# One gather per natural tile and a destination part expanded from h in a graph network kernel

## The reference

```
h = relu(layernorm(x))
fwd = [h[dst], h[src], ea];  bwd = [h[src], h[dst], ea]      # 80 features
msg = relu([fwd; bwd] @ Wf1 + bf1) @ Wf2 + bf2
flow[dst] += msg of fwd;  flow[src] += msg of bwd
x = x + relu(flow @ Wn1 + bn1) @ Wn2 + bn2
h = relu(layernorm(x))
out = x + segment_sum(h[dst], src)
```

## Time and profile before

| | us |
|---|---|
| median of 3 runs | 7432.28 (7426.3 to 7452.46) |
| the profiled execution | 7458.13 |
| its span, first to last instruction | 7456.5 |
| start, to the first DVE work on an edge tile | 186.4 |
| edge stage | 4310.6 |
| record sums | 808 |
| node network | 105 |
| neighbour sums | 2046 |

### The profile page before, as it was taken

The page is one execution under the profiler, slowest core; times in us unless marked ns, Lnnn a source line. Parts: engine busy times, 40 slices in busy tenths (PEclk is TensorE's granted clock), DMA queues, the critical chain, the costliest instruction groups (busy, mean ns, idle before and its releaser), DMA issues.

```text
span 7456.5 us, 123779 instructions
## 1 busy us (share of the span) xinstructions
PE 5573.1 (75%) x24859; PEld 4715.3 (63%) x24860; DVE 3152.5 (42%) x14104; ACT 933.8 (13%) x3532; POOL 5306.1 (71%) x5865
## 2 busy tenths in 40 slices
PE   4898989898989999989898998999833333333334
PEld 3677767677777777767777778999723333333334
DVE  4444444444444444444444445666522232223223
ACT  2111111111111111111111113444200000000000
POOL 0777777777777777777777776666267777777774
PEclk8766676766666666676666665555555555555555
DMA  5111111111111111111111113333121111111111
GB/s 143 43 42 42 42 42 42 42 42 42 42 42 42 41 41 41 41 41 41 41 41 41 41 41 71 73 71 73 21 23 15 14 15 15 14 15 15 15 14 18
DMA packets 916520, 294.53 MB, mean 39 GB/s; under 512 B 795687, under 2 KB 864597, under 8 KB 915822
## 3 DMA queue, kind: packets, MB, share of 16 engines
q0 software_dynamic: 156896, 189.98, 10.1%
q1 hardware_dynamic: 759102, 91.68, 9.0%
q10 hardware_dynamic: 336, 11.20, 0.5%
HBM read 227.82 MB, written 82.32 MB: 42 GB/s over the span
## 4 chain that ended last, share of the span: by engine, by line
POOL 56%; issue 28%; PE 6%; DVE 5%; DVEq 2%; DMA 2%; POOLq 1%; ACT 0%; ACTq 0%; SPq 0%
POOL t L663 19%; POOL records L612 18%; POOL g L602 18%; DVE acc L1186 3%; PE bank L947 1%; PE bank L1002 1%; DVEq L318 1%; DVE oht L1255 1%; DVE ohd L1255 1%; PE bank L809 1%; PE bank L972 1%; PE bank L895 1%; PE bank L894 1%; DVEq L1186 0%; DMA rec_i<-by_d_sd 0%
## 5 line engine op out<-in xcount | busy, mean ns | idle before, releaser
L602 POOL DMA_INDIRECT g<-t_rows,rec_i x1664 | 1615.6, 971 | 625.7 <-issue 505.6
L612 POOL DMA_INDIRECT records<-rec,pos x1664 | 1671.7, 1005 | 518.0 <-issue 501.7
L663 POOL DMA_INDIRECT t<-h_rows,didx x1568 | 1491.0, 951 | 603.8 <-issue 475.6
L1002 PE MATMUL bank<-t,ohd 128*128 x1664 | 376.2, 402 | 1315.1 <-DMA t<-h_rows,didx 1315.1
L893 PE MATMUL bank<-g,ident 128*128 128x128 f32 x3328 | 926.0, 373 | 376.6 <-DMA g<-t_rows,rec_i 376.4
L1002 PEld LDWEIGHTS bank<-t,ohd 128*128 128x128 f32 x1664 | 362.9, 330 | 1328.0 <-issue 1327.8
L895 PE MATMUL bank<-t,oht 128*128 x3328 | 1136.9, 438 | 0.0
L894 PE MATMUL bank<-wee,eaT 17*128 17x128 f32 x3328 | 1120.4, 429 | 0.0
L1195 DVE TENSOR_TENSOR prod<-bank,q_row 128x392 f32<-128x392 f32 x416 | 235.7, 567 | 2086.5 <-PE bank L910 2085.1
L893 PEld LDWEIGHTS bank<-g,ident 128*128 128x128 f32 x3328 | 738.7, 274 | 397.8 <-issue 396.6
L1186 DVE TENSOR_TENSOR acc<-acc,bank 128x65 f32 x3328 | 733.8, 220 | 513.8 <-issue 325.3
(11 more groups left out here) (203 smaller groups left out, 6492.0 us busy)
## 6 DMA issues: line engine op xcount, KB each, us to landing
t<-records SPq DMA_DIRECT2D x104, 536.0 KB, 4.2
rec_i<-by_d_sd SPq DMA_DIRECT2D x1664, 1.0 KB
eaT<-by_d_ea SPq DMA_DIRECT2D x1664, 8.0 KB
g<-t_rows,rec_i POOLq DMA_INDIRECT x1664
records<-rec,pos POOLq DMA_INDIRECT x1664
t<-h_rows,didx POOLq DMA_INDIRECT x1568
by_d_ea<-in_ea ACTq DMA_DIRECT2D x7, 1562.5 KB, 22.1
t_rows<-t2s SPq DMA_DIRECT2D x26, 256.0 KB, 2.3
```

Source lines behind the costliest of these rows:

```text
L602: nc.gpsimd.indirect_dma_start(out=g2[:, r, u, :], out_offset=None, in_=t2_rows, in_offset=bass.IndirectOffsetOnAxis(ap=rec_i[:, r, u, 0:1 ...
L612: nc.gpsimd.indirect_dma_start(out=records, out_offset=bass.IndirectOffsetOnAxis(ap=pos[:, r, u:u + 1].bitcast(U32), axis=0), in_=rec[:, r ...
L663: nc.gpsimd.indirect_dma_start(out=h2g[:, w * W + t, :], out_offset=None, in_=h2_rows, in_offset=bass.IndirectOffsetOnAxis(ap=didx[:, k, t ...
L1002: ins = nc.tensor.matmul(s_bank[r][:, u * D:(u + 1) * D], s_oh[r][:, u, :], h2g[:, bass.ds(at[r * U + u], 1), :].rearrange("p a f -> p (a ...
```

## The change

- t1 is gone. The normalised h is kept as three bf16 parts beside each other (h3, 96 columns for a node: the rounded value, the rounded rest, the rounded rest of that). A new step, expand, multiplies the transposed one-hot with the block of h3; ACT copies the 96 rows from PSUM into rows 0 to 95 of cmb, whose other rows are a row of ones and the 16 edge features. One product cmb x w3 then gives the destination part, the bias and the edge part.
- t2 rows are gathered by the natural tiles (1568) with indices loaded for a whole window (sidx) into a ring of 128 tiles; hidden reads a tile from its slot in the ring.
- The destination one-hot is made by DVE in bf16, by four instructions instead of one, and transposed by PE in bf16. ACT copies it to f32 for sums.
- PE transposes round r + 2 at the end of round r; before it transposed round r + 1 behind hidden of round r.
- x is loaded first from an array laid out by the host, and normalised before the work on the edges; the histogram is moved among the tables; 28 small weight loads become 7; ACT starts the copy of the edge features before the tables, in pieces of 125 elements instead of 1000.
- The neighbour sums are added to x itself, and the copy of x before that stage (L778) is gone.

The diff, cut:

```diff
+H3 = 3 * D
+RG = 8 * W
+NTW = TW
...
-        t1 = sb("t1", [P, NBP, P])
+        h3 = sb("h3", [P, NBP, H3], BF16)
+        ring_flat = sb("ring", [P, RG * P])[:, :]
+        ring = ring_flat.rearrange("p (t c) -> p t c", c=P)
...
-        g2 = sb("g2", [P, R, U, P])
+        sidx = sb("sidx", [P, 8, W, 2], I32)
+        ohd_h = sb("ohd_h", [P, 2, U, P], BF16)
...
-            def load_edges(i, first, last):
+            def load_sources(i, m):
+                sp.dma_start(sidx[:, m, :, :], by_d_sd[bass.ds(i * (W * P), W * P), :].rearrange("(t p) k -> p t k", p=P)).then_inc(ld_nat[m], 16)
+
+            def load_edges(i, m, first, sources):
+                if sources:
+                    load_sources(i + 1, (m + 1) % 8)
...
-            def gather_t2(i, r):
-                pool.wait_ge(ld_sd[r], 16 * U * (i + 1))
-                pool.sem_inc(pool_tick, 1)
+            def gather_t2(s, m, r):
+                if r == 0:
+                    pool.wait_ge(ld_nat[m], 16 * (s + 1))
+                    pool.sem_inc(pool_tick, 1)
                 for u in range(U):
                     nc.gpsimd.indirect_dma_start(
-                        out=g2[:, r, u, :], out_offset=None, in_=t2_rows,
-                        in_offset=bass.IndirectOffsetOnAxis(ap=rec_i[:, r, u, 0:1].bitcast(U32), axis=0)).then_inc(gat[r], 16)
+                        out=ring[:, m * W + r * U + u, :], out_offset=None, in_=t2_rows,
+                        in_offset=bass.IndirectOffsetOnAxis(ap=sidx[:, m, r * U + u, 0:1].bitcast(U32), axis=0)).then_inc(gat[r], 16)
...
-            def edges(i, first, last):
-                for r in range(R):
-                    if r < R - 2:
-                        gather_t2(i, r + 2)
-                    elif not last:
-                        gather_t2(i + 1, r + 2 - R)
-                    scatter_records(i, r)
-            gather_t2(0, 0)
-            gather_t2(0, 1)
-            rounds(pool, edges)
+            def edges(s, gathers):
+                for m in range(8):
+                    for r in range(R):
+                        m2, r2 = m + (r + 2) // R, (r + 2) % R
+                        if m2 < gathers:
+                            gather_t2(s + m2 // 8, m2 % 8, r2)
+                        scatter_records(s * 8 + m, r)
+            gather_t2(0, 0, 0)
+            gather_t2(0, 0, 1)
+            edges(0, 9)
+            with pool.Fori(1, NTW // 8) as s:
+                edges(s, 9)
+            edges(NTW // 8, NTW % 8)
...
             def transposed(i, r):
                 v = i * R + r + 1
                 act.wait_ge(tp_ready, v)
-                nc.scalar.activation(oht[:, r % 2, :, :].rearrange("p u n -> p (u n)"), pb[0][:, :], ACT.Copy).then_inc(oht_ready, 1)
+                nc.scalar.activation(oht_h[:, r % 2, :, :].rearrange("p u n -> p (u n)"), oht_ps, ACT.Copy).then_inc(oht_ready, 1)
+
+            def expanded(i, r):
+                v = i * R + r + 1
+                act.wait_ge(hd_ps, v)
+                act.sem_inc(act_tick, 1)
+                nc.scalar.activation(cmb[0:H3, r, :, :].rearrange("p u n -> p (u n)"), pb[1][0:H3, :], ACT.Copy).then_inc(cmb_ready, 1)
+                act.wait_ge(ohd_ready, v)
+                act.sem_inc(act_tick, 1)
+                nc.scalar.activation(ohd[:, r % 2, :, :], ohd_h[:, r % 2, :, :], ACT.Copy).then_inc(ohd32_ready, 1)
 
...
                     hidden(i, r, first)
                     if r < R - 1:
-                        transposed(i, r + 1)
+                        expanded(i, r + 1)
                     elif not last:
-                        transposed(i + 1, 0)
+                        expanded(i + 1, 0)
+                    if r < R - 2:
+                        transposed(i, r + 2)
+                    elif not last:
+                        transposed(i + 1, r + 2 - R)
...
-            def transposes(i, r, very_first=False):
+            def transposes(i, r):
                 v = i * R + r + 1
-                if not very_first:
-                    pe.wait_ge(oht_ready, v - 1)
-                    pe.sem_inc(pe_tick, 1)
                 pe.wait_ge(ohd_ready, v)
+                pe.sem_inc(pe_tick, 1)
                 for u in range(U):
-                    ins = nc.tensor.transpose(pb[0][:, u * P:(u + 1) * P], ohd[:, r % 2, u, :], ident[:, :])
+                    ins = nc.tensor.transpose(oht_ps[:, u * P:(u + 1) * P], ohd_h[:, r % 2, u, :], ident_h[:, :])
                 ins.then_inc(tp_ready, 1)
 
-            def hidden(i, r):
-
+            def expand(i, r, very_first=False):
                 v = i * R + r + 1
                 at = four(pe, blk[1], i * W + r * U, NB)
-                pe.wait_ge(gat[r], 16 * U * (i + 1))
+                if not very_first:
+                    pe.wait_ge(cmb_ready, v - 1)
+                    pe.sem_inc(pe_tick, 1)
+                pe.wait_ge(oht_ready, v)
                 pe.sem_inc(pe_tick, 1)
+                for u in range(U):
+                    ins = nc.tensor.matmul(pb[1][0:H3, u * P:(u + 1) * P], h3[:, bass.ds(at[u], 1), :].rearrange("p a c -> p (a c)"), oht_h[:, r % 2, u, :],
+                                           start=True, stop=True)
+                ins.then_inc(hd_ps, 1)
+
+            def hidden(i, r, gathered):
+
+                v = i * R + r + 1
+                at = four(pe, gs_row, i * W + r * U, RG - 1)
+                if gathered:
+                    pe.wait_ge(gat[r], 16 * U * (i + 1))
+                    pe.sem_inc(pe_tick, 1)
                 pe.wait_ge(ld_ea[r], 16 * U * (i + 1))
                 pe.sem_inc(pe_tick, 1)
-                pe.wait_ge(oht_ready, v)
+                pe.wait_ge(cmb_ready, v)
+                pe.sem_inc(pe_tick, 1)
                 for u in range(U):
                     p = pb[2][:, u * P:(u + 1) * P]
-                    nc.tensor.matmul(p, ident[:, :], g2[:, r, u, :], start=True, stop=False)
-                    nc.tensor.matmul(p, eaT[:, r, u, :], wee[:, :], start=False, stop=False)
-                    ins = nc.tensor.matmul(p, oht[:, r % 2, u, :], t1[:, bass.ds(at[u], 1), :].rearrange("p a c -> p (a c)"), start=False, stop=True)
+                    nc.tensor.matmul(p, ident[:, :], ring[:, bass.ds(at[u], 1), :].rearrange("p a c -> p (a c)"), start=True, stop=False)
+                    ins = nc.tensor.matmul(p, cmb[:, r, u, :], w3[:, :], start=False, stop=True)
                 ins.then_inc(pre_ready, 1)
...
+                pe.sem_inc(pe_tick, 1)
+                pe.wait_ge(ohd32_ready, v)
                 for u in range(U):
                     ins = nc.tensor.matmul(pb[3][:, u * ACC:(u + 1) * ACC], ohd[:, r % 2, u, :], rf[:, u, :], start=True, stop=True)
                 ins.then_inc(sum_ready, 1)
 
-            def edges(i, first, last):
+            def edges(i, first, last, gathered=True):
                 for r in range(R):
-                    hidden(i, r)
+                    hidden(i, r, gathered)
                     if r < R - 1:
-                        transposes(i, r + 1)
+                        expand(i, r + 1)
                     elif not last:
-                        transposes(i + 1, 0)
+                        expand(i + 1, 0)
                     counts(i, r, first)
                     sums(i, r, first)
-            transposes(0, 0, True)
-            rounds(pe, edges)
+                    if r < R - 2:
+                        transposes(i, r + 2)
+                    elif not last:
+                        transposes(i + 1, r + 2 - R)
...
+            dve.wait_ge(x_in, 16)
+            dve.wait_ge(tails_set, 1)
+            centre(own, xs, slice(0, NBP), ln_tmp)
+            scale_relu(var_ready, std_ready).then_inc(h_ready, 1)
+
             dve.wait_ge(nat_in, 32)
...
-                nc.vector.tensor_tensor(ohd[:, r % 2, :, :], bcast_mid(iota128[:, :], U), bcast(dloc, P), ALU.is_equal).then_inc(ohd_ready, 1)
+                for u in range(U):
+                    ins = nc.vector.tensor_scalar(ohd_h[:, r % 2, u, :], iota_h[:, :], dloc[:, u:u + 1], None, ALU.is_equal)
+                ins.then_inc(ohd_ready, 1)
...
+    w12 = np.zeros((P, U, P), np.float32)
+    for u in range(U):
+        w12[u * D:(u + 1) * D, u, :] = np.concatenate([second, first], axis=1)
+    as_dst = np.concatenate([first, second], axis=1)
...
```

More of the change, by code:

```diff
@@ L774, in _, with histogram @@
             nc.scalar.activation(stat[:, 1, :], stat[:, 1, :], ACT.Sqrt).then_inc(std2_ready, 1)
-            act.wait_ge(x1_done, NG)
-            nc.scalar.activation(acc2[:, :, :], xs[:, :, :], ACT.Copy).then_inc(acc2_set, 1)
         @block.tensor
         def _(pe):
-            for m in range(2):
+            def histogram(m):
                 pe.wait_ge(hot_ready, m + 1)
@@ L853, in _ @@
                              start=True, stop=True).then_inc(ncol_ps, 1)
-            tables(8, False, False)
             pe.wait_ge(ncol_ready, 1)
```

328 lines of the change are left out of this document (177 added, 151 removed).

## The result

| | before | after |
|---|---|---|
| median, us | 7442.37 (4 runs) | 7537.08 (4 runs, 7528.39 to 7554.61) |
| ratio after / before | | 1.0132, 95% interval 1.0102 to 1.0163 |
| profiled execution, us | 7458.13 | 7543.88 |
| start | 186.4 | 180.3 |
| edge stage, and per round | 4310.6, 10.36 | 4401.7, 10.58 |

A forecast was written before the change was run, and what follows sets the result against it. POOL set the mean pace before; afterwards a PE-DVE-PE ring of 11.65 us a round would bind. 416 rounds make 4846 us, +536; with 42 off the start and 26 to the median, 7458.1 becomes 7926, range 7740 to 8240.

The forecast's parts named there:

- The ring: Edge stage: PE, DVE and PE wait for each other within every round; 11.8 us at 1.2 GHz.
- step 2: Edge stage, DVE: from positions to the start of the one-hot, same instructions as before; 3.35 us a round.
- Fewer gathers: POOL: 96 gathers less at 1.296 us, 124 us, counting only where POOL sets the pace.
- Less PE work: Hidden on PE: the edge-feature product goes, 0.72 us a tile, so hidden falls to 4.6 us at 1.2 GHz.
- Counts: Edge stage: from the first counts product on PE to positions on DVE; 1.39 us a round at 1.2 GHz.
- A: Rival: 2.4 GHz in most edge-stage rounds, POOL's pace of 10.37 us holds; 7384 us in all; chance 0.13.
- The four one-hots: Edge stage, DVE: four bf16 instructions of 128 columns; 0.54 us a round, plus 0.12 for contention with POOL.
- Step 4: Edge stage, PE: from ohd_ready to the next hidden, with transposes, register load and waits; 1.3 us a round.
- The start: Before the edge stage: first edge work near 144 us instead of 186.4; gain 42 us, bounds 20 and 65.
- B: Rival: a third of edge-stage rounds at 2.4 GHz, 10.8 us a round; 7572 us in all; chance 0.12.
- POOL under 65%: Sign of being right: POOL waits for the relu or positions, its busy share under 65%.
- PEclk under 0.55: Sign of being right: PEclk 0.5 to 0.55 in the edge stage, about one round in twenty at 2.4 GHz.

The follow-up runs named there:

- e5_cmb17: The changed kernel with the second product of hidden cut to 17 rows, destination part left out; 9525.42 us, ratio 1.035 to the kernel before.
- e6_b113: The kernel before with its edge product padded from 17 to 113 rows by zeros; 9157.19 us, ratio 0.996 to the kernel before.
- e7_fill: The changed kernel with eight unread bf16 products on PE between sums and transposes; 9424.03 us, ratio 1.026 to the kernel before.
- e3_start: The changed kernel with the edge-feature copy on ACT behind the tables again, in pieces of 1000; 9366.41 us, ratio 1.027 to the kernel before.
- a_again: The changed kernel, unaltered, run again on another chip; 9444.04 us, ratio 1.028 to the kernel before on that chip.

## Why the prediction was right in its direction and wrong in its size

*What held.* The ring and its place, the wait before the transposes, step 2 to 0.03 us, the neighbour and record sums unchanged. Fewer gathers gained nothing, as POOL no longer set the pace, if by little: its share of the stage fell from 76% to 72%.

*What failed: "Less PE work", the term 4 x (1.87 - 0.72) = 4.6 us.* The 0.72 us was read as the whole price of the edge product, and the other two products were to keep their 1.15 us. But the 17 rows had slowed these too: the three pairs of a tile start 0.56, 0.72 and 0.59 us apart with them, and 0.43 each in the kernel with 113 rows. So the two that stay take 0.855 us, not 1.15, and what leaves is 1.87 - 0.855 = 1.01 us a tile. The rows to see it in were there: in the earlier trace rows the four transposes, f32 products of 128 rows and 128 columns with none of 17 rows among them, take 0.86 us (2004.52 to 2005.38), 0.215 us each, where the six products of a tile of hidden take 0.31 each. Hidden was forecast at 4.6 us and measured 3.53, which is -1.07 us a round, 445 us of the stage; e5_cmb17 and e6_b113 show the cause. It alone brings the forecast from 6.6% to 0.7%.

*Smaller terms.* Counts 0.98 instead of 1.39 (-0.41): they follow hidden and are at 2.4 GHz in 70% of the rounds (under 1 us; in 20% they take the forecast's 1.3 to 1.4), where I had one round in twenty. The clock is neither A's nor the forecast's: hidden at 1.2 GHz (never under 3.2 us, where e7_fill has 1.88 at 2.4), counts and sums mostly at 2.4, PEclk 0.69 over the stage. Expand 0.33 instead of 0.5 (-0.17). The four one-hots 0.76 instead of 0.66 with contention (+0.10); the contention isn't seen, as they take 0.74 us (median) beside POOL's DMAs and 0.74 the two times that POOL stood idle. What was too short is the start every 0.12 us. Step 4 1.60 instead of 1.3 (+0.30). The prediction said of a round under 11.2 that step 4 would have been too dear; the round was 10.58, and step 4 was too cheap. Together 11.8 - 1.07 - 0.41 - 0.17 + 0.03 + 0.10 + 0.30 = 10.58.

*The start*, 42 forecast and 6 measured: the bounds of 20 and 65 did not hold it. The work counted was right to 7 us (151.1 in e3_start against 144), and the copy of the edge features, now early and in 500-byte pieces, was counted only as a gain; SP's queue stands behind it for 40.62 us. e3_start gives 29 of the 36 us back.

By the profiled execution: 7952 - 444 of stage + 36 of start = 7544, as measured.

*The rivals.* B is nearest in time (7572) but not in kind: it wanted a third of all rounds fast. The signs listed were mixed: PE idle before the transposes, right; POOL under 65%, wrong, because the ring came out 0.5 us above POOL's mean need instead of 1.6 (10.58 and 11.65 against 10.07); PEclk under 0.55, wrong, because counts and sums ran at 2.4 GHz.

## What to carry to other kernels

Price a removed product by its neighbours too: look whether the weight loads around it run ahead, and compare the tile with and without it at the same number of rows. When a wait closes a ring between two engines, move the work that is waited for to where its engine idles; here the same four instructions, put before positions, are worth 2 us a round while POOL doesn't gather. And look how far the next limit is: on the first chip POOL stands at most 0.5 us behind. Before a copy is started early, ask which queue stands behind it and how long its pieces are.

## What the hardware showed that was not expected

Between f32 products of 128 rows, one of 17 rows keeps the weight loads around it from running ahead. At 1.2 GHz, pairs start 0.725 us apart where every second product has 17 rows (e5_cmb17), and 0.56, 0.72 and 0.59 where every third has (before), against 0.43 with 113 rows in either kernel. Five chips took 23 or 24% longer for the same kernel. There DVE's start behind PE's counts came 3.8 us late in the median of a_again while POOL issued its DMAs (0.04 us on the first chip, with the same DMAs), though the instructions in the rows above are as long on both. And PE's clock rises and falls within a round: hidden at 1.2 GHz, the counts, 3.9 us after hidden's start, at 2.4 in 70% of the rounds.
